# Products of probabilities with values: two groups of four head groups instead of four groups of two

## What is computed

```python
x = x + retention(layernorm(x), ...)                 # stage A
q, k, v = (layernorm(x) @ Wq + bq), (ctx @ Wk + bk), (ctx @ Wv + bv)
scores = einsum('bhqd,bhkd->bhqk', q, k) * scale     # stage B, 16 heads of 16
attn = softmax(where(causal, -inf, scores))
x = x + einsum('bhqk,bhkd->bhqd', attn, v) @ Wo + bo
x = x + gelu(layernorm(x) @ w1[e] + b1[e]) @ w2[e] + b2[e]   # stage C, e = pair of sequences
```

## Time and profile before

| | before |
|---|---|
| median of 3 runs | 359.83 us |
| profiled execution | 359.76 us |
| its span | 358.0 us |
| TensorE products busy | 335.6 us, 94% of the span |
| TensorE weight loads busy | 278.3 us, 78% |
| VectorE busy | 263.8 us, 74% |
| ScalarE busy | 239.8 us, 67% |
| GpSimd busy | 157.5 us, 44% |
| granted TensorE clock | full in all 40 slices |
| chain that ended last | TensorE 74%, issue 9%, VectorE 8%, ScalarE 4%, GpSimd 3% |

### The profile page before, as it was taken

How to read it: one execution, slowest core, us unless ns; L and a number is a source line. 1 busy time by engine, 2 the same in 40 slices (tenths; PEclk the granted TensorE clock), 3 DMA queues, 4 the chain that set the end, 5 groups by cost and what they waited for, 6 DMA issues and landing times.

```text
span 358.0 us, 8965 instructions
## 1 busy us (share of the span) xinstructions
PE 335.6 (94%) x3283; PEld 278.3 (78%) x3283; DVE 263.8 (74%) x552; ACT 239.8 (67%) x585; POOL 157.5 (44%) x144
## 2 busy tenths in 40 slices
PE   7788798999999999999999999999999999989797
PEld 3556466987889878888889878887889877758696
DVE  5665666698768976798668976798667967584784
ACT  4362655588857867578757868579757877697451
POOL 4246251263733657163743657163743651732010
PEclk9999999999999999999999999999999999999999
DMA  5950100304014220404014120404005300404000
GB/s 143 295 210 1 32 2 2 146 2 146 4 40 153 72 78 6 164 23 146 0 15 176 53 93 0 150 40 146 0 15 179 104 15 16 148 1 135 2 29 29
DMA packets 22313, 26.95 MB, mean 75 GB/s; under 512 B 2896, under 2 KB 20112, under 8 KB 22288
## 3 DMA queue, kind: packets, MB, share of 16 engines
q1 hardware_dynamic: 21472, 26.52, 23.4%
q10 hardware_dynamic: 816, 0.10, 0.2%
HBM read 24.51 MB, written 2.10 MB: 74 GB/s over the span
## 4 chain that ended last, share of the span: by engine, by line
PE 74%; issue 9%; DVE 8%; ACT 4%; POOL 3%; DMA 1%; ACTq 0%; DVEq 0%; POOLq 0%
PE c L1209 19%; PE a L1209 15%; PE b L1209 15%; PE b1k L1209 7%; PE b1k L1366 6%; PE b2k L1209 3%; DVE probT L916 2%; PE c L1393 2%; PE a L1224 1%; DVE scD L890 1%; DMA wk_c<-in_L_attn_Wk 1%; PE b2k L1224 1%; PE c L1224 1%; DVE negmax L909 1%; PE b L1224 1%
## 5 line engine op out<-in xcount | busy, mean ns | idle before, releaser
L463 POOL TENSOR_TENSOR w_lo<-w_in,w_hi 128x512 fp32r<-128x512 f32 x28 | 39.2, 1420 | 31.2 <-ACT w_hi L555 27.2
L593 ACT ACTIVATE prob<-b,negmax 128x128 f32<-128x128 f32 x124 | 35.9, 388 | 21.4 <-DVE negmax L909 21.4
L1366 PE MATMUL b1k<-ident,prob 128*128 128x128 f32 x256 | 39.4, 276 | 5.7 <-DVE probT L916 2.7
L450 POOL TENSOR_TENSOR rstA<-varA,minus_half 128x16 f32<-128x16 f32 x8 | 23.4, 2926 | 45.4 <-DVE varA L1048 45.4
L457 POOL TENSOR_TENSOR w_lo<-w_in,w_hi 128x512 fp32r<-128x512 f32 x28 | 34.9, 1279 | 12.9 <-ACT w_hi L555 11.2
L555 ACT ACTIVATE w_hi<-w_in 128x512 fp32r<-128x512 f32 x64 | 38.6, 641 | 2.6 <-PE b L1209 2.6
L1366 PEld LDWEIGHTS b1k<-ident,prob 128*128 128x128 f32 x256 | 28.7, 141 | 11.8 <-issue 6.0
L916 DVE COPY probT<-b1k 128x512 f32<-128x512 f32 x32 | 22.0, 689 | 14.4 <-PE b1k L1366 14.4
L1209 PE MATMUL c<-xTC_hi,w_hi 128*128 128x256 f32 x108 | 31.9, 296 | 0.5
L902 DVE TENSOR_TENSOR h_lo<-h_in,h_hi 128x512 fp32r<-128x512 f32 x32 | 30.7, 959 | 1.1
L450 POOL TENSOR_TENSOR rsC<-mvC,minus_half 128x2 f32<-128x2 f32 x8 | 5.7, 710 | 57.6 <-DVE mvC L846 57.6
(11 more groups left out here) (296 smaller groups left out, 1121.1 us busy)
## 6 DMA issues: line engine op xcount, KB each, us to landing
w_in<-in_L_ffn_w SPq DMA_DIRECT2D x16, 1024.0 KB, 5.4
x_in<-in_x SPq DMA_DIRECT2D x8, 256.0 KB, 2.9
c_in<-in_ctx SPq DMA_DIRECT2D x8, 256.0 KB, 2.9
out<-x2b SPq DMA_DIRECT2D x7, 256.0 KB, 2.2
b_cur<-in_L_ffn_b SPq DMA_DIRECT2D x8, 128.0 KB, 3.0
W_sb<-in_L_attn_W SPq DMA_DIRECT2D x2, 256.0 KB, 4.7
decay_sb<-in_decay SPq DMA_DIRECT2D x1, 512.0 KB, 3.9
h_in<-in_L_xattn_Wk SPq DMA_DIRECT2D x1, 256.0 KB, 4.9
```

The lines of the kernel that those rows point to most:

```text
L450: pool.tensor_tensor(out, in_, minus_half[:, 0:n], ALU.pow).then_inc(s_out, 1)
L463: pool.tensor_tensor(w2_lo[:, part, :], w2_in[:, part, :], w2_hi[:, part, :].bitcast(F32), ALU.subtract).then_inc(s_w2lo, 1)
L593: ins = nc.scalar.activation(prob[:, u % PR, g, :], score_banks[u][:, g * P:(g + 1) * P], ACT.Exp, bias=negmax[:, u, g:g + 1], scale=-1.0)
L1366: ins = nc.tensor.transpose(b1k[:, g * P:(g + 1) * P], prob[:, u % PR, g, :], ident[:, :])
```

## The change

It only moves calls in TensorE's program. `with_values(0)` and `with_values(1)` no longer stand behind `scores(1)`, and `with_values(2)` and `with_values(3)` no longer behind `prob_transposes(4)`: all four stand behind `down(5)`, ahead of `prob_transposes(4)`. `with_values(4)` to `with_values(7)` stand together behind `down(7)`. No instruction is added, none is taken away, and the programs of the other engines are as they were.

```diff
                 if do_b:
                     scores(1)
-                    with_values(0)
-                    with_values(1)
                 if do_c:
                     down(4)
...
                 if do_c:
                     down(5)
                 if do_b:
+                    for u in range(PR):
+                        with_values(u)
                     prob_transposes(4)
-                    with_values(2)
-                    with_values(3)
...
                 if do_b:
                     prob_transposes(6)
-                    with_values(4)
-                    with_values(5)
...
                 if do_c:
                     down(7)
                 if do_b:
-                    with_values(6)
-                    with_values(7)
+                    for u in range(PR, 2 * PR):
+                        with_values(u)
                 if do_b and nextA:
                     pe.wait_ge(s_pTd, 4 * (b + 1))
                     context(b1k)
```

## The result

The changed kernel takes 363.57 us (median of 6 executions, 362.35 to 364.02) against 359.84 us (6, 359.76 to 361.05). The ratio is 1.0083, with a 95% interval of 1.0062 to 1.0105: 0.8% slower. The profiled execution of the changed kernel took 362.35 us, with a span of 360.6 us, so between the two profiles there are 2.6 us. The rest of the difference of the medians is not the change's: two of the six executions before and four of the six after took 1.2 to 1.7 us more than the shortest of their kernel, and with nine idle products in step 9 no execution of either kernel does (experiments 9 and 10: 2.55 us between the medians).

A forecast was written before the change was run, and what follows sets the result against it. It took ScalarE's queue between the copies of groups 4 and 6 as the bound, TensorE just filling it. Terms 2.15 + 1.38 - 0.2, together +3.3 us on 359.76, gave 363.1 us, range 361.4 to 363.9.

The forecast's parts named there:

- down(4) sooner, group 4 later: TensorE, loop step: down(4) 0.57 us sooner, group of four 1.01 us, transpositions of group 4 0.20 us later.
- All that was won is waited away ahead of group 5: Ahead of group 5, TensorE waits for ScalarE's copy of group 4; nothing moves from there to group 6.
- The copy of group 6 binds, with a new wait ahead of group 7: ScalarE's queue ends this copy later; TensorE stalls about 1 us, group 7 starts 0.22 to 0.31 us later.
- it is ScalarE's queue that sets the time: Kernel before, from group 4's to group 7's transpositions: ScalarE, busy 5.82 of 5.83 us, was said to be the bound.
- copy of group 6 later, 0.22 + 4 x 0.29 = 1.38 us: Later start of group 7 over five steps: 0.22 us in step 2, 0.29 in each of four others.
- The group of four behind down(7) costs 0.43 us a step: with_values(4 to 7) grow that group from 0.58 to 1.01 us, in five steps, 2.15 us.
- Step 1 -0.2 us, step 7 nothing: Step 1: ScalarE is free, group 7's copy 0.2 us sooner; step 7: the later end is covered by the xnB wait, 0.
- Fewer switches pay: Rival: ScalarE no bound, the step is TensorE's alone, -0.8 us a step, 355.6 us; chance 0.09.
- Only the cover is lost: Rival: ScalarE's queue has hidden slack, only 0.43 us a step remain, 361.7 us; chance 0.12.

The follow-up runs named there:

- experiment 9: The kernel before with nine idle products added in step 9: 359.67 us median, ratio 0.9982.
- experiment 10: The changed kernel with nine idle products added in step 9: 362.22 us median, ratio 1.0054 to the kernel before.
- experiment 1: Against the kernel before, only with_values(0 to 3) together behind down(5), pairs 4, 5 and 6, 7 left in place: 40.62 us a step, 361.38 us, ratio 1.0024.
- experiment 3: The changed kernel with ScalarE's copy of head group 6 moved ahead of the last rounding: 40.59 us a step, 361.53 us, ratio 1.0028 to the kernel before.
- experiment 4: The kernel before with ScalarE's copy of head group 6 moved ahead of the last rounding: 40.46 us a step, 360.27 us, ratio 0.9990.
- experiment 5: Kernel before with with_values(0 to 3) together behind down(5), and down(6) moved ahead of prob_transposes(5): 40.62 us a step, 361.07 us, ratio 1.0013.
- experiment 11: Kernel before with with_values(4 to 7) together, pv_out(0) behind the first rounding, GpSimd's first w1_low waiting for xnA: 40.83 us a step, 361.69 us, ratio 1.0044.
- experiment 2: Against the kernel before, only with_values(4 to 7) together behind down(7), pairs 0, 1 and 2, 3 left in place: 40.94 us a step, 362.86 us, ratio 1.0071.
- experiment 6: experiment 5 with ScalarE's copy of head group 6 also ahead of the last rounding: 40.10 us a step, 358.42 us, ratio 0.9922 to the kernel before.
- experiment 8: experiment 6 with nine idle products added in step 9: 357.18 us median, ratio 0.9899 to the kernel before.
- the swap: On ScalarE, the copy of head group 6 ahead of the last rounding; alone in the kernel before (experiment 4): 40.46 us a step, 360.27 us.
- experiment 7: Kernel before with with_values(4 to 7) together behind down(7) and ScalarE's pv_out(0) moved behind the first rounding: 41.64 us a step, 366.50 us, ratio 1.0162.

## Why the prediction was right, and where it was off

It said slower, 363.1 us, in a range of 361.4 to 363.9. The profiled execution took 362.35 us, the median is 363.57.

- *down(4) sooner, group 4 later.* Right to 0.01 us: 0.31 us from the 32-row products to `down(4)` (measured 171.54 - 171.24 = 0.30), 1.01 us for the group of four (174.60 - 173.59), and group 4 0.19 us later in the step.
- *All that was won is waited away ahead of group 5.* Right: 4.71 us behind `scores(1)`, at the early end of the forecast; group 6 0.05 us sooner than before.
- *The copy of group 6 binds, with a new wait ahead of group 7.* Right in mechanism for the changed kernel, shown by experiments 1, 3, 4 and 5. For the kernel before, "it is ScalarE's queue that sets the time" was too strong: by experiment 4 it was a tie with TensorE's own work in the loop steps. (The copy of group 6 there ends at 179.34 + 0.66 = 180.00, not 179.99; nothing hangs on it.) **The size was off:** the term "copy of group 6 later, 0.22 + 4 x 0.29 = 1.38 us" came out at about 0.10 us a step, 0.5 us. Two things were in it. ScalarE's queue got the products of `pvT` long before it needed them, where before it had to wait for them, and so took 5.05 us instead of the 5.18 read from the earlier trace rows: the 0.60 us from the copy to `pvT` there held 0.11 us of waiting that no idle time marks. Experiment 11 shows those 0.11 us by themselves. And group 7 started 0.06 us behind the end of the copy (181.07 against 180.35 + 0.66 = 181.01), as in step 4 of the kernel before, and not 0.15 us behind it. In step 2 it is 0.14 us after the change too (98.97 against 98.17 + 0.66), so there the slip is 0.10 us by the shorter queue alone, where 0.22 was forecast.
- *The group of four behind down(7) costs 0.43 us a step.* Right: experiment 2, 40.94 - 40.51.
- *Step 1 -0.2 us, step 7 nothing.* Right: the retention of step 2 comes 0.18 us sooner, 80.80 against 80.98, and from the retention of step 7 on the two profiles run alike to 0.04 us.
- Sum by the measured terms: 5 x 0.43 + 5 x 0.10 + 5 x 0.01 (what the step has beyond the two) - 0.2 = 2.5 us, and the two profiles lie 2.6 us apart. The medians lie 3.7 us apart, and with the idle products 2.55. By that the change alone gives about 362.4 us, 0.7 us below the forecast and inside its range; that the measured median lies above 363.1 instead is the longer executions, which the prediction did not reckon with. Two of the four had a mean granted clock of 0.995; the two at 364.0 us had one of 1.00 and a span of 362.2 us, and what made them longer is open.
- *Rivals.* Fewer switches pay: false for this kernel, but the saving is real, and experiments 6 and 8 collect it for the first four, together with the covered wait for VectorE. The Trainium skill, TensorEngine Tiling (Array Packing), Key Properties, says that changing the tiling mode drains the engine; the trace agrees that a separate group costs something, 1.01 us for 32 instructions against 2 x 0.57 for two groups of 16. In the change, what was won ahead of group 5 went into a wait. Only the cover is lost: nearer than its chance of 0.12 made it, since only 0.10 of the 0.54 us a step is the slip, and 0.43 is the bigger group behind `down(7)`, all that this rival kept.

## What to carry to other kernels

Small groups that interrupt an engine may be the cover for another engine's turnaround; before they are put together, write down for each buffer handed over (transpose, copy, next transpose) how much work stands in between, and what is left after the move. A queue on another engine that is busy without a gap can be the bound, or tie with it, even if that engine's share of the span is 67%; a saving on the first engine ahead of it isn't seen until that queue is relieved too (against experiment 1, `down(6)` by itself brought 0 us a step, and with the swap 0.52 us; the swap by itself was tried only in the kernel before, 0.05 us, and in the changed one, 0.47 us). When an instruction is moved on one engine, look at what a third one starts because of it: the 0.6 us by which a rounding came sooner cost 0.8 us a step.

## What the runs showed of the hardware that was not expected

**VectorE and GpSimd on SBUF.** A VectorE instruction of 0.41 us (scale and shift of 128x256 f32, SBUF to SBUF) took 1.42 us when a GpSimd subtraction of 1.28 us had begun ahead of it, and ended 0.15 us behind the end of that one; with GpSimd started behind it, it took 0.41 us again (experiments 7 and 11). By the Trainium skill, SBUF — State Buffer, section SBUF: two separate sides, the two engines share a port pair, which a GpSimd instruction or one of certain kinds of VectorE instruction holds to its end once it has started, while the other one is blocked. The trace agrees, 1.42 us against 0.41. It also shows that not every VectorE instruction is held: outT, which reads one of its operands from PSUM, ran beside the next GpSimd subtraction in 0.86 us for two instructions, and takes 0.87 us in the kernel before.

**The clock behind the last wait.** In step 9 TensorE waits 2.46 us for VectorE's xnC, in the kernel before at 337.7 to 340.2 us. In the profiled executions of experiments 1, 3, 4, 6 and 11, which don't have the nine products, the clock falls, in 1, 6 and 11 by the end of that wait and in 3 and 4 about 1 us behind it; in experiment 4's the granted clock is 0.66 in the mean from 340 to 345 us, that is for some two thirds of it at the lower of its two levels (1.2 GHz) and for the rest at 2.4 GHz. The profiles of before and after the change and of experiments 2, 5 and 7 don't have it, though TensorE waits there as long. Busy times in stretches, experiment 4's profile, then experiment 9's:

```profile
335.00:340.00 5.00, 2.54 (x23) 2.34 (x22) 3.96 (x13) 0.56 (x2) 1.20 (x2) 1.00 0.00 0
340.00:345.00 5.00, 5.00 (x32) 5.00 (x31) 3.81 (x6) 0.90 (x2) 1.09 (x1) 0.66 0.01 3
```

```profile
335.00:340.00 5.00, 4.59 (x31) 3.29 (x31) 3.84 (x11) 1.14 (x3) 0.81 (x1) 1.00 0.01 3
340.00:345.00 5.00, 4.81 (x39) 4.61 (x40) 4.97 (x10) 1.55 (x3) 1.47 (x1) 1.00 0.00 0
```

In the second TensorE is busy 4.59 of 5 us with the idle products in the wait, and the clock stays. The 30 executions of the four kernels with the nine products lie within 0.4 us of the others of their kernel; those of the kernels without them spread over 1.3 to 3 us, but for the four of experiment 2 (0.4), none of which is undisturbed. Not all of that spread is seen in the clock: some executions with a mean of 1.00 are longer too, in the span (two of the changed kernel, by 1.6 us) or around it (up to 3.7 us instead of 1.8). None of the 30 is. Why the clock falls in one execution and not in the next, and how the others come by their time, was not tried.
